# The roll layer's pipeline in groups of two images in place of four

## The reference

```python
h = h + _L0_ffn_ref(_layernorm(h), ...)      # 64 experts, 8 per token, and a shared expert
h = h + _L1_attn_ref(_layernorm(h), ...)     # the roll layer
h = h + _L1_ffn_ref(_layernorm(h), ...)      # 8 experts, 1 per token

def _L1_attn_ref(x, W_A, W_V, W_O, b_O):     # x: image, token, 256;  16 heads of 16
    z = softmax(einsum('bse,he->bsh', x, W_A) * 16 ** -0.5, axis=1)   # over the tokens
    roll = z.transpose(0, 2, 1)[:, :, (i - j) % S] * (j <= i)         # causal convolution
    v = einsum('bse,fe->bsf', x, W_V).reshape(B, S, H, D)
    out = einsum('bhij,bjhd->bihd', roll, v).reshape(B, S, E)
    return einsum('bse,fe->bsf', out, W_O) + b_O
```

## Time and profile before

| | |
|---|---|
| Median of three runs | 1091.64 us (1090.90 to 1091.76) |
| Span of the profiled execution, first to last instruction | 1089.2 us (no time of its own is listed for it) |
| PE busy / its weight loads | 945.4 us (87%) / 754.5 us (69%) |
| DVE, ACT, POOL busy | 585.3, 419.2, 536.6 us |
| Mean granted TensorE clock | 0.943 of full |
| Roll layer with the shared expert, 651.4 to 893.4 us | 242 us, 22% of the span |

### The profile page before, as it was taken

How to read it: one execution, slowest core, us unless ns; L and a number is a source line. 1 busy time by engine, 2 the same in 40 slices (tenths; PEclk the granted TensorE clock), 3 DMA queues, 4 the chain that set the end, 5 groups by cost and what they waited for, 6 DMA issues and landing times. The chain is left out here.

```text
span 1089.2 us, 29445 instructions
## 1 busy us (share of the span) xinstructions
PE 945.4 (87%) x10292; PEld 754.5 (69%) x10318; DVE 585.3 (54%) x1439; ACT 419.2 (38%) x1094; POOL 536.6 (49%) x714
## 2 busy tenths in 40 slices
PE   8689999988845699999999988489999964999996
PEld 6557777766734588888888878245566543888895
DVE  1678877775699377633333333678877433111111
ACT  2246666661417244434344321223333221433331
POOL 0056666650230777777677726777773002333332
PEclk9889999998988799999999999689999995999998
DMA  7000000000100879887788833334554038466750
GB/s 249 17 28 3 0 0 0 0 2 30 54 1 1 309 247 285 249 263 236 223 279 257 251 113 92 101 103 123 142 172 181 20 102 305 136 207 236 288 152 25
DMA packets 79820, 149.28 MB, mean 137 GB/s; under 512 B 18892, under 2 KB 53327, under 8 KB 75760
## 3 DMA queue, kind: packets, MB, share of 16 engines
q1 hardware_dynamic: 34768, 77.15, 20.9%
q0 software_dynamic: 17712, 47.88, 15.6%
q10 hardware_dynamic: 27248, 23.09, 6.3%
HBM read 200.22 MB, written 31.73 MB: 213 GB/s over the span
## 5 line engine op out<-in xcount | busy, mean ns | idle before, releaser
L1308 POOL DMA_INDIRECT x_x<-m_x_rows,x_idx x170 | 166.0, 977 | 74.6 <-POOL x_idx L1293 35.4
L1334 PE MATMUL x_pup<-x_xt,x_w 128*128 128x128 f32 (+1 forms) x2176 | 184.1, 251 | 0.0
L1334 PEld LDWEIGHTS x_pup<-x_xt,x_w 128*128 128x128 f32 (+1 forms) x2176 | 168.1, 165 | 5.8 <-issue 5.7
L1603 POOL DMA_INDIRECT rl_y<-m_y_rows,rl_idx x136 | 132.3, 973 | 45.5 <-issue 36.9
L1404 DVE TENSOR_TENSOR x_hid<-x_gate,x_pup 128x128 f32<-128x128 f32 x170 | 48.9, 288 | 148.6 <-ACT x_gate L1376 142.4
L1348 PE MATMUL x_pdown<-x_w,x_hid 128*128 128x256 f32 (+1 forms) x408 | 104.2, 389 | 0.2 <-DVE x_y L1411 0.2
L1372 ACT ACTIVATE x_xt<-x_pturn 128x256 f32<-128x256 f32 x170 | 65.3, 384 | 89.0 <-PE x_pturn L1319 85.6
L423 POOL TENSOR_TENSOR wa_probs<-wa_probs,wa_peak 68x544 f32<-68x544 f32 x64 | 70.9, 1108 | 57.7 <-DVE wa_peak L569 57.7
L2362 DVE TENSOR_TENSOR x_y<-x_pdown,x_b 128x256 f32<-128x256 f32 x21 | 8.9, 425 | 151.1 <-PE x_pdown L2318 151.1
L2348 ACT ACTIVATE x_hid<-x_pup,x_b 128x128 f32<-128x128 f32 (+1 forms) x200 | 52.9, 356 | 93.8 <-PE x_pup L2301 93.7
L1376 ACT ACTIVATE x_gate<-x_pup 128x128 f32<-128x128 f32 x170 | 47.2, 278 | 92.9 <-PE x_pup L1334 92.9
(11 more groups left out here) (329 smaller groups left out, 1939.3 us busy)
## 6 DMA issues: line engine op xcount, KB each, us to landing
x_w<-in_experts SPq DMA_DIRECT2D x204, 384.0 KB
late_w<-in_w SPq DMA_DIRECT2D x28, 1024.0 KB, 13.1
m_y_rows<-x_y ACTq DMA_DIRECT2D x170, 128.0 KB, 2.4
xT<-in_w SPq DMA_DIRECT2D x12, 1024.0 KB, 6.0
xn<-in_w SPq DMA_DIRECT2D x10, 1024.0 KB, 10.7
h<-in_w SPq DMA_DIRECT2D x10, 1024.0 KB, 14.5
m_x_rows<-xn SPq DMA_DIRECT2D x34, 128.0 KB, 1.9
x_x<-m_x_rows,x_idx POOLq DMA_INDIRECT x170
```

The lines of the kernel that those rows point to most:

```text
L1308: nc.gpsimd.indirect_dma_start(x[:, s, :], None, x_rows, bass.IndirectOffsetOnAxis(ap=idx[:, s:s + 1], axis=0))\
L1334: mm = nc.tensor.matmul(pup[rows:rows + wide, bank, m * P + side * wide:m * P + (side + 1) * wide], w[:, lane, first:first + wide], xt[:, ...
L1603: nc.gpsimd.indirect_dma_start(y[:, t % YR, kk, :], None, y_rows, bass.IndirectOffsetOnAxis(ap=idx[:, n:n + 1], axis=0))\
```

## The change

Six things change together.

- `GI = 2`: 16 groups of two images, 136 columns each. A step brings in one tile (two the first time) and lets out one (two the last time). There are 19 steps in place of 11.
- The inner index `p` is gone: a group is what half a group was. `values`, `forward`, `multiply`, `invert`, `move_values` and `move_out` run once a step. The matmuls of each are the same ones. Instructions that spanned a group (`mix_logits`, `turn_mix`, `forward_mix`, the softmax, `root`, the moves of the mix, `add_projected`) are twice as many and half as wide.
- The order within a step is new on PE, ACT and DVE, and the last steps have no order of their own.
- `fill` and `fill_mid` are gone; a step has five filling matmuls (two in `fill_mix`, three in `fill_values`), where a step of four images had 17. The last three steps have at most those of group 15; steps 17 and 18 have none.
- The gathers are paced only by the shared expert (the first 18 after gather 0) and by the ring. The semaphore of a ring place is split in two, so `combine` may start on the first four rows of a tile. It runs in three pieces of 4, 2 and 2 instructions, with `mix_shift` and `mix_norm` between them, and tile 0 is combined in part inside the shared expert's loop.
- SP's four loads stand ahead of group `NG - 8` of 16, again behind outgoing tiles 0 to 7.

```diff
-    GI = 4
+    GI = 2
...
     def tiles_in(g):
         if not 0 <= g < NG:
             return []
-        return list(range(0 if g == 0 else 2 * g + 1, 2 * g + 3))
+        return [0, 1] if g == 0 else [g + 1]
...
-        return list(range(2 * g, NT if g == NG - 1 else 2 * g + 2))
+        return [g, g + 1] if g == NG - 1 else [g]
...
-        y_in = ring_sems(nc, k, "rl_y_in", YR)
+        y_in = ring_sems(nc, k, "rl_y_in", 2 * YR)
...
-                    if g == NG - 4:
+                    if g == NG - 8:
...
-                        if t >= YR:
-                            g = max(0, (t - YR - 1) // 2)
-                            if t - YR == tiles_in(g)[-1]:
-                                first_half(g, kk)
-                            elif g:
-                                second_half(g, kk)
...
-                            .then_inc(y_in[t % YR], 16)
+                            .then_inc(y_in[t % YR * 2 + kk // YH], 16)
...
                     if has2:
-                        forward(g2, 0, 0)
-                        forward(g2, 0, 1)
-                        forward(g2, 1, 0)
+                        forward(g2, 0)
+                        forward(g2, 1)
                     for t in tiles_in(g1):
                         turn("in", t)
-                        fill(g1, 1)
                     if has1:
-                        fill(g1, 1)
                         mix_logits(g1)
-                        values(g1, 0)
+                        values(g1)
                     if has2:
-                        forward(g2, 1, 1)
...
+                        invert(g2)
                     for t in outs:
                         turn("out", t)
-                        fill_mid(g1, 1)
                     if has1:
-                        values(g1, 1)
+                        fill_mix(g1, 2)
+                        fill_values(g1, 2)
+                    if has2:
+                        project(g2)
                     for t in outs:
                         choose(t)
...
                     if has1:
                         turn_mix(g1)
-                    for m, ts in pairs_out(g2):
-                        project(g2, m, ts)
-                    if has1:
-                        fill_values(g1, 2)
+                        fill_values(g1, 1)
                         forward_mix(g1)
-                        fill_values(g1, 2)
...
+                for n in range(LATE + 2):
+                    if n < LATE:
+                        shared_hidden(n)
+                    if n >= 2:
+                        shared_add(n - 2)
+                    if n in (7, 8):
+                        combine(0, (n - 7) * 3, (n - 7) * 3 + 3)
+                dve.wait_ge(sh_added, LATE)
+                combine(0, 6, K0)
+                measure_in(0)
```

228 lines of the change are left out of this document (74 added, 154 removed).

## The result

The changed kernel takes 1081.51 us, the median of four runs (1080.58 to 1082.33). The kernel before took 1091.27 beside it (1089.75 to 1091.76, four runs). The ratio is 0.9904, with a 95% interval of 0.9886 to 0.9923. The forecast was 1078.2 with a range of 1072 to 1089: right in sign and within the range, 3.3 us too low. The execution profiled after has a span of 1080.6 and a time of 1082.33.

What follows compares the result with a forecast made beforehand. PE's own work list and short waits bound the steady part. Head about 4 us, shorter pipeline and end about 9, steady rate nothing: 13.4 less, span 1075.8, plus 2.4 makes 1078.2; range 1072 to 1089.

Steps and rivals of the forecast that it cites:

- Steady rate: Full pipeline steps: 11.1 us for two images, 22.2 for four against 22.17 before, so no change.
- The balance behind it: Steady step: five fillers in place of 8.5 give back 0.8 us, and serial ways over ACT cost as much.
- Head: Start of the layer: first `root` near 685 instead of 692.7, step 1 7.5 us earlier; gives about 4.
- Drain: Layer's end: 18.4 us from step 3's 14 intervals on; shorter pipeline and one tile fewer give about 9.
- Sum of the layer: Layer's end at 880.0 in place of 893.4, so 13.4 us less.
- The rest of the program: Code behind the layer: all of the next layer is queued behind its end, so the whole gain carries through.
- (a): Steady step: the DVE and ACT chain becomes the bound, steps 11.5 to 12, 1084 to 1091 us; chance 0.16.
- (b): Steady step: TensorE clock drops within steps, slower than before, 1116 us with one fall per step; chance 0.05.
- (c): Gathers become the bound at the slowest row's rate, ending 10 us later: 1088 us; chance 0.06.
- (d): Steady step: PE loses its idle bits, 10.2 to 10.7 us a step: 1066 to 1073 us; chance 0.08.
- (e): Next function: the gain is real but lost there, its loads and routing not having waited: 1091 us; chance 0.03.
- Edits costed at nothing: SP's four loads and POOL's dropped waits worth nothing; split semaphore and combine in pieces matter only at tile 3.

Runs made afterwards that it cites:

- fill_as_before: The changed kernel with 8.5 filling matmuls a step in place of 5, as many per image as the kernel before: 1086.63 us, ratio 0.9958.
- head_fill: The changed kernel with 36 filling matmuls on PE ahead of the pipeline's first step: 1074.19 us, ratio 0.984.
- late_tile0: The changed kernel with tile 0 combined wholly behind the shared expert's loop, as before: 1083.06 us, ratio 0.9911.
- drain_fill: The changed kernel with filling matmuls in the last two steps, ahead of the last inversion and around the last transposes: 1072.63 us, ratio 0.9829.
- no_fill: The changed kernel without its five filling matmuls per step: 1072.88 us, ratio 0.9843.
- head_drain: The changed kernel with the added fillers of both head_fill and drain_fill, its five per steady step kept: 1071.97 us, ratio 0.9838.
- gathers_free: The changed kernel with the first 18 gathers freed from waiting for the shared expert's products: 1080.25 us, ratio 0.9896.
- combo: head_drain without filling matmuls in the steady steps from group 2 on, their waits still issued: 1074.29 us, ratio 0.9873.
- final: combo with one wait where the steady fillers stood, and SP's loads ahead of group 12 in place of 8: 1071.56 us, ratio 0.982.
- before_free: The kernel before without POOL's waits on PE for the gathers from tile 4 on: 1092.04 us, ratio 0.9998.
- whole_combine: The changed kernel with each tile's eight additions in one piece ahead of the softmax, from tile 2 on: 1081.28 us, ratio 0.993.

## Why the prediction held, and where not

- **Steady rate** (forecast 11.1 a step, "does not change"): 10.77. The windows of PE's list were right to 0.12 up to the outgoing transpose. Two terms were too large: a `project` is 1.29 and not 1.40 where its input is long there (802.81 to 804.10), and `turn_mix` to `forward_mix` takes 0.52 and not 0.7. That is 14 x 0.33 = 4.6 us too much. The balance behind it was right in kind. Five fillers in place of 8.5 give back 0.77 a step (fill_as_before; forecast 0.8), and the new structure, with the ways over ACT that a second half used to cover, costs 0.45, not "as much". "The steady rate nothing" is thereby wrong: a step gains 0.32, and fewer fillers, which the prediction set off against the structure, are 11.5 of the gain.
- **Head** (first `root` near 685, step 1 7.5 earlier): 33.58 after the layer's start against 41.35, so 7.8. The instant of step 3, forecast 54.8 after the start, came at 54.55. The low clock there cost what was allowed for, and head_fill shows 2.3 of it. Of the 7.8 late_tile0 gives 2.6 to tile 0's early additions.
- **Drain** (18.4 from the last `forward_mix`): 21.5, from 858.92 to 880.40. This is the term that was mis-sized. The prediction let the clock fall only before the last transposes, at 0.6. It fell before `invert`, behind an idle stretch of 1.81 that the sum contained without saying so, and `invert` and the two `project`s took 4 us more than forecast (1.8 and 2.2); the writes took 1.2 less than forecast (4.5 from the first to the end, not 5.7). drain_fill gave 4.05 back.
- **Sum of the layer**: forecast end 880.0, measured 880.40. The steps gave 4.6 more and the drain 3.1 less than forecast, and the layer began 2.2 later. So the agreement of the end is partly luck.
- **The rest of the program** was held to be rigid. It was 4.4 longer in the profile, at a wait for a bias that varies from one execution to the next. This, less the 0.6 by which the allowance of 2.4 was too large, is what parts 1078.2 from 1081.51.
- **Rivals.** (a), the chain over DVE: not here, with 0.51 of reserve (forecast 0.6), but it has come level with PE in no_fill at 10.33. (b), the clock within steps: 1.00 in all steady windows at idles up to 0.47. The Trainium skill, "TensorE: Matmul & The Clock Gate", section "A second HAM failure mode: psum-queue depth-cycling", tells of an engine that idles for moments between groups of matmuls and swings between its levels; this kernel's steady part does not, while single idles of 1.8 us, in the drain and at no_fill's start, were each followed by half speed. But in one step of head_drain the clock fell to half speed with no idle over 0.57 in the 17 us before. That short idles bring no fall is what the steady parts show here, and not a rule. (c), the gathers: not in this kernel, and gathers_free gained nothing; it came true in combo and final, where the lead is short and loads run beside the gathers. (d), lost idle bits: half true, 10.77 against a range of 10.2 to 10.7. (e), a gain lost behind the layer: 4.4 of 15.2 in this profile, at the wait for the bias. The prediction gave (e) 0.03 and left this out of its sum; whether the change has a share in it is not shown.
- **Edits costed at nothing**: POOL's pacing (before_free), the pieces of the combine (whole_combine) and SP's loads at 1.01 share are all worth nothing here. That combines do not wait in the steady part of the kernel before was misread: DVE waits there for gathered rows, 1.95 at 750.05 and 0.81 at 815.27, but the steps stay 22.18, so the cost of nothing stands. The early combine of tile 0 is worth 2.6 of the root and up to 3.2 of the layer.

## What to carry to other kernels

Finer groups in a pipeline can pay at its ends, not in its rate: here the structure gained 5.4 us although each step was 0.45 longer, and most of these 5.4 belong to tile 0's early additions and to the clock in the drain. The rate was won only by leaving out fillers. So test a change of group size with the number of fillers held fixed. Put fillers where a stage is missing (head, first steps, drain) and take them, with their waits, from where every stage is full. When a head or a step gets faster, look next at what had lived off its slack: here the lead of the gathers over 4 MB of loads, which took back 4.9 us in combo, and 6.8 of the 12.6 us that final would have had over the changed kernel (226.86 - 214.2) when the loads had been moved.

## What the runs showed of the hardware

- A filler of 0.22 us costs less than 0.22 where a wait stands behind it: 5 a step cost 0.44 together (10.77 against 10.33), and 7 in the step of before 0.75 in most steps. Where none does it costs all of it: 3.5 more a step cost 0.77.
- Waits that, by the order of ACT's moves, are already satisfied cost PE time: two of them, at places without a filler, made a step 0.21 longer (10.54 in combo against 10.33 in final).
- The clock stayed full at idles of 0.47 us a step for 150 us; idles of 1.80, 1.81 and 2.34 us between stretches of work were followed by work at the lower level, that of 1.04 was not. The same idle does not give the same fall: behind 1.81 us, 64 passes took 3.90 us at half speed in one kernel, and 2.54 in another, where the clock fell only as they ended. And with equal idles, none over 0.57, the clock fell in head_drain's second step (0.57 as the mean of 697.5 to 701.5) and stayed full in combo's.
- Loads of 4 MB at a DMA share of 1.01 to 1.03 delay gathered rows by enough for waits of 2.3 and 2.2 us, with steps of 12.5 to 14.0 instead of 10.3 to 10.5; with a larger lead (8.2 us in no_fill and 11.2 in the changed kernel, from a tile's last gather to the addition that may need it, against 4.0 and 3.7) the same loads cost nothing.
